# Layer 2 of a two-layer image kernel on one Trainium2 core: variances on 64 columns, and the pass towards the states reordered with its spreading step moved to GpSimd

## What is computed

```python
def _layer_norm(x, g, b):
    mu = jnp.mean(x, axis=-1, keepdims=True)
    var = jnp.mean((x - mu) ** 2, axis=-1, keepdims=True)
    return (x - mu) * jax.lax.rsqrt(var + EPS) * g + b

def _s5_block(x, i, ...):                       # x: (batch, 65536 pixels, 64 channels)
    fx = _layer_norm(x, ln1_g[i], ln1_b[i])
    h = _s5_scan(fx, ...)                       # B-matrix, a complex scan both ways, C-matrix, D * fx
    x = jax.nn.gelu(h) + fx
    fx2 = _layer_norm(x, ln2_g[i], ln2_b[i])
    return fx2 @ ff_enc[i].T @ ff_dec[i].T + fx2

x = x + _L0_conv_ref(_gn(x), ...)               # layer 1
x = x + _L1_conv_ref(_gn(x), ...)               # layer 2: _s5_block by rows and by columns, fused
```

## Time and profile before

| what | value |
|---|---|
| median of 3 runs | 9685.14 us (9671.85 to 9687.74) |
| the profiled execution | 9676.74 us, span 9674.9 us |
| TensorE busy | 8792.1 us, 91% of the span, 81958 matmul instructions |
| VectorE busy | 8178.5 us, 85% |
| ScalarE busy | 5402.5 us, 56% |
| GpSimd busy | 1604.1 us, 17% |
| mean granted TensorE clock | 0.958 of full speed |

### The profile page before, as it was taken

One profiled execution on the slowest core, in us unless ns is written; L12 is line 12 of the kernel. 1 busy time (PEld: TensorE's weight loads), 2 busy tenths in 40 slices (PEclk: granted clock), 3 DMA queues, 4 the chain that ended last, 5 costly groups with the idle time before them and its releaser, 6 DMA issues.

```text
span 9674.9 us, 203022 instructions
## 1 busy us (share of the span) xinstructions
PE 8792.1 (91%) x81958; PEld 5941.5 (61%) x81958; DVE 8178.5 (85%) x11463; ACT 5402.5 (56%) x8539; POOL 1604.1 (17%) x1824
## 2 busy tenths in 40 slices
PE   1799989999899998998989999899998999889998
PEld 1566655656566665565656666565565666656565
DVE  7799989888788988888869999887986888888786
ACT  0455546566655555556765555645675555465666
POOL 0000002333300000333320000122341000023333
PEclk6899999999999999999999999999999999999999
DMA  4777766585677777658578777756767777675755
GB/s 107 169 169 170 169 153 224 180 256 153 164 172 168 167 168 185 199 167 260 153 168 174 170 166 171 226 159 192 214 175 156 155 155 155 144 237 172 243 167 155
DMA packets 1370032, 1719.03 MB, mean 178 GB/s; under 512 B 849788, under 2 KB 1081356, under 8 KB 1283852
## 3 DMA queue, kind: packets, MB, share of 16 engines
q1 hardware_dynamic: 1369100, 1706.04, 68.9%
HBM read 852.77 MB, written 514.86 MB: 141 GB/s over the span
## 4 chain that ended last, share of the span: by engine, by line
PE 51%; SPq 19%; DMA 11%; DVE 11%; issue 4%; ACT 2%; POOL 0%; DVEq 0%; ACTq 0%; POOLq 0%
PE ps L1781 14%; SPq L788 11%; DMA H<-P 10%; PE ps L1794 7%; PE ps L1805 5%; PE ps L868 5%; PE ps L1429 3%; PE ps L882 3%; SPq L780 2%; SPq L732 2%; DVE S L1563 2%; SPq L722 2%; PE ps L1355 2%; PE ps L1388 2%; PE ps L931 2%
## 5 line engine op out<-in xcount | busy, mean ns | idle before, releaser
L1174 DVE SCALAR_TENSOR_TENSOR F<-U,LW,F 106x512 f32<-106x512 f32 x2048 | 1537.8, 751 | 63.6
L1781 PE MATMUL ps<-fp,Dwr 128*128 128x512 f32 x6144 | 1549.1, 401 | 1.9 <-DVE tt L1549 1.9
L1781 PEld LDWEIGHTS ps<-fp,Dwr 128*128 128x128 f32 x6144 | 1114.8, 188 | 618.6 <-ACT x L1870 291.3
L868 PE MATMUL ps<-P,WP 128*128 128x512 f32 x3072 | 922.4, 422 | 52.0 <-DMA H<-P 50.4
L1870 ACT ACTIVATE x<-ps,cst 128x512 f32<-128x512 f32 x512 | 352.2, 688 | 1037.2 <-PE ps L1794 1033.1
L1794 PE MATMUL ps<-XP,Cwr 128*128 128x512 f32 x3072 | 805.7, 399 | 82.4 <-DVE XP L1916 82.4
L868 PE MATMUL ps<-H,WP 128*128 128x512 f32 x3072 | 811.9, 399 | 0.0
L1042 ACT ACTIVATE xr<-P 64x1024 fp32r<-64x1024 f32 x512 | 544.0, 1063 | 475.9 <-DVE P L1143 462.1
L1927 DVE SCALAR_TENSOR_TENSOR x<-fx,g,x 128x512 f32<-128x512 f32 x512 | 382.9, 748 | 467.4 <-ACT x L1870 466.6
L1429 PE MATMUL ps<-fp,Bwr 128*128 128x512 f32 x3072 | 776.8, 403 | 0.4 <-DVE tt L1549 0.4
L1092 POOL TENSOR_SCALAR xo<-xo 64x512 f32<-64x512 f32 x4 | 6.0, 1499 | 4522.0 <-DVE xo L1208 4522.0
(11 more groups left out here) (302 smaller groups left out, 17895.0 us busy)
## 6 DMA issues: line engine op xcount, KB each, us to landing
H<-P SPq DMA_DIRECT2D x512, 585.0 KB, 7.3
raw<-x SPq DMA_DIRECT2D x240, 640.0 KB, 9.2
fx_d<-fx SPq DMA_DIRECT2D x112, 1024.0 KB, 6.6
fl_d<-fp SPq DMA_DIRECT2D x112, 1024.0 KB, 7.0
fp<-fl_d SPq DMA_DIRECT2D x112, 1024.0 KB, 6.9
fx<-fx_d SPq DMA_DIRECT2D x112, 1024.0 KB, 5.3
XT<-xT SPq DMA_DIRECT2D x256, 256.0 KB, 7.5
x1h_d<-xo SPq DMA_DIRECT2D x256, 256.0 KB, 9.2
```

What stands on the lines that cost most here:

```text
L868: e.matmul(ps[2 + i][:], w(pw_, W_CONV + 128 * j, 128), m, start=(j == 0 and pw_ == 0 and px == 0), stop=False)
L1174: ins = e.scalar_tensor_tensor(o, u, wd[0:106, i:i + 1], o, ALU.mult, ALU.add)
L1781: ins = e.matmul(bank(m)[:], Dwr[:, w, c:c + 128], fq[n % 2][x][:, s2, :], start=(s2 == 0 and w == 0 and x == 0), stop=False)
```

## The change

- `variances`: each piece's 512 columns are now cut into eight parts of 64. Two matmuls of 64 columns, with two halves of a wider `En`, fill all 32 rows of a strip where one matmul of 128 columns filled 16. The tile of a group is 128 x 64, in pass A and in pass B. The number of these matmuls doubles, their columns halve.
- the square root, `deviations` and `deviations_b` work on 64 columns in place of 128. `deviations` writes its result into a tile of its own, `rr`.
- `blocks` leaves ScalarE and becomes one `tensor_tensor` of 128 x 512 on GpSimd, ahead of the turn and the sums there.
- pass A's order on three engines: TensorE puts `bc` 0 and 1 between the first two parts of `bmm`, ahead of `center(g, 2)`, and `bc` 2 and 3 behind it; VectorE puts `norm` 0 and 1 between the two `rotate`; ScalarE does `round_` 0 and 1 behind `xcsq` 1, and `round_` 2 and 3 behind `xcsq` 3.

```diff
     def variances(e, o, i, src, pick):
-        for q in range(4):
-            ins = e.matmul(o[32 * q:32 * q + 32, 0:128], pick[:, 32 * i:32 * i + 32], src[:, 128 * q:128 * q + 128],
-                           start=(i == 0), stop=(i == 3))
+        for h in range(2):
+            for q in range(4):
+                c = 128 * q + 64 * h
+                ins = e.matmul(o[32 * q:32 * q + 32, 0:64], pick[:, 128 * h + 32 * i:128 * h + 32 * i + 32], src[:, c:c + 64],
+                               start=(i == 0 and h == 0), stop=(i == 3 and h == 1))
...
-    def deviations(e, own, done, value, out):
-        e.wait_ge(sem[done], value)
+    def deviations(e, own, f, g):
+        e.wait_ge(sem["sd"], NG * f + g + 1)
         own(e.reciprocal(rs[:], rs[:]))
         own(e.tensor_copy(rh[:], rs[:]))
-        e.scalar_tensor_tensor(rs[:], rh[:].bitcast(F32), lows, rs[:], ALU.mult, ALU.add).then_inc(sem[out], 1)
+        if g:
+            e.wait_ge(sem["rd"], NG * f + g)
+        e.scalar_tensor_tensor(rr[:], rh[:].bitcast(F32), lows, rs[:], ALU.mult, ALU.add).then_inc(sem["rs"], 1)
...
         for g in range(NG + 2):                       # TensorE
             center(g, 0)
             bmm(g - 2, 0)
+            bc(g - 1, 0)
+            bc(g - 1, 1)
             bmm(g - 2, 1)
             center(g, 2)
-            for i in range(4):
-                bc(g - 1, i)
+            bc(g - 1, 2)
+            bc(g - 1, 3)
             bmm(g - 2, 2)
             bmm(g - 2, 3)
             var(g)
...
         for g in range(NG + 1):                       # ScalarE
             xcsq(g, 0)
             xcsq(g, 1)
-            blocks(g - 1)
+            round_(g - 1, 0)
+            round_(g - 1, 1)
             xcsq(g, 2)
-            for i in range(4):
-                round_(g - 1, i)
             xcsq(g, 3)
+            round_(g - 1, 2)
+            round_(g - 1, 3)
...
-                e.activation(rs[:], ps[2][:, 0:128], ACT.Sqrt, bias=eps[:]).then_inc(sem["sd"], 1)
+                e.activation(rs[:], ps[2][:, 0:64], ACT.Sqrt, bias=eps[:]).then_inc(sem["sd"], 1)
...
             rotate(g - 3, 0)                          # VectorE
+            norm(g - 1, 0)
+            norm(g - 1, 1)
             rotate(g - 3, 1)
...
-            for i in range(4):
-                norm(g - 1, i)
+            norm(g - 1, 2)
+            norm(g - 1, 3)
             part(g - 1, 0)
             part(g - 1, 2)
             scan(g - 3)
...
     def pa_pool(e, b, d):
         f = phase(b, d)
+
+        def blocks(g):
+            e.wait_ge(sem["rs"], NG * f + g + 1)
+            if g:
+                e.wait_ge(sem["bc"], M * f + 4 * g)
+            e.tensor_tensor(RD[:].rearrange("k (q c) -> k q c", q=8), rr[:].bitcast(F32).unsqueeze(1).to_broadcast([128, 8, 64]),
+                            own_q.unsqueeze(2).to_broadcast([128, 8, 64]), ALU.mult).then_inc(sem["rd"], 1)
+
+        blocks(0)
+        blocks(1)
         for g in range(NG):
+            if g + 2 < NG:
+                blocks(g + 2)
             if g:
                 turn_pool(e, f, g - 1, slice(0, 64), 512 * g + 1, d)
```

More of the change, by code:

```diff
@@ L93, in constants @@
     k["k_ctr"] = (p[:, None] // 64 == p[None, :] // 64) * ((p[:, None] == p[None, :]) - 1.0 / 64)
-    e = np.zeros((128, 4, 32))
-    b = np.zeros((4, 32, 4, 4, 128))
-    mask = np.zeros((4, 32, 1))
+    e = np.zeros((128, 2, 4, 32))
+    b = np.zeros((8, 16, 4, 128))
+    mask = np.zeros((8, 16, 1))
     for par in range(2):
@@ L100, in constants @@
                 r = 4 * i + 2 * c + par
-                e[par * 64:par * 64 + 64, i, r] = 1.0 / 64
-                for q in range(4):
-                    b[q, r, i, q, par * 64:par * 64 + 64] = 1.0
+                for h in range(2):
+                    e[par * 64:par * 64 + 64, h, i, 16 * h + r] = 1.0 / 64
+                b[:, r, i, par * 64:par * 64 + 64] = 1.0
                 mask[:, r] = -c
-    k["k_E"] = np.concatenate([e.reshape(128, 128), mask.reshape(128, 1), np.kron(np.eye(4), np.ones((32, 1)))], 1)
-    k["k_Bc"] = np.concatenate([b.sum(3).reshape(128, 512), np.roll(b.sum(3), 64, 3).reshape(128, 512)], 1)
+    k["k_E"] = np.concatenate([e.reshape(128, 256), mask.reshape(128, 1), np.kron(np.eye(8), np.ones((16, 1)))], 1)
+    k["k_Bc"] = np.concatenate([b.reshape(128, 512), np.roll(b, 64, 3).reshape(128, 512)], 1)
     k["k_id"] = 1.0 * (p[:, None] % 64 == np.arange(64)[None, :])
@@ L135, in build @@
     ctq = at("ctq", [128, 128])
-    En, Bc = at("En", [128, 133]), at("Bc", [128, 1024], F32R)
-    lows, own_q = En[:, 128:129], En[:, 129:133]
+    En, Bc = at("En", [128, 265]), at("Bc", [128, 1024], F32R)
+    lows, own_q = En[:, 256:257], En[:, 257:265]
     RR = at("RR", [128, 2])
@@ L246, in build @@
     tiny = at("tiny", [128, 4])
-    rs = at("rs", [128, 128])
-    rh = at("rh", [128, 128], F32R)
+    rs = at("rs", [128, 64])
+    rh = at("rh", [128, 64], F32R)
+    rr = at("rr", [128, 64], F32R)
+    offset[0] += 256
     RD = at("RD", [128, 512], F32R)
@@ L1349, in deviations_b @@
         own(e.scalar_tensor_tensor(rs[:], rh[:].bitcast(F32), lows, rs[:], ALU.mult, ALU.add))
-        e.tensor_tensor(RD[:].rearrange("k (q c) -> k q c", q=4), rs[:].unsqueeze(1).to_broadcast([128, 4, 128]),
-                        own_q.unsqueeze(2).to_broadcast([128, 4, 128]), ALU.mult).then_inc(sem[out], 1)
+        e.tensor_tensor(RD[:].rearrange("k (q c) -> k q c", q=8), rs[:].unsqueeze(1).to_broadcast([128, 8, 64]),
+                        own_q.unsqueeze(2).to_broadcast([128, 8, 64]), ALU.mult).then_inc(sem[out], 1)
     def variances(e, o, i, src, pick):
-        for q in range(4):
-            ins = e.matmul(o[32 * q:32 * q + 32, 0:128], pick[:, 32 * i:32 * i + 32], src[:, 128 * q:128 * q + 128],
-                           start=(i == 0), stop=(i == 3))
+        for h in range(2):
+            for q in range(4):
+                c = 128 * q + 64 * h
+                ins = e.matmul(o[32 * q:32 * q + 32, 0:64], pick[:, 128 * h + 32 * i:128 * h + 32 * i + 32], src[:, c:c + 64],
+                               start=(i == 0 and h == 0), stop=(i == 3 and h == 1))
         return ins
@@ L1479, in round_ @@
             e.activation(piece(fp[g % 2][0], i, d), piece(fx[g % 2], i, d), ACT.Copy).then_inc(sem["f1"], 1)
[L1481 to L1489, removed]
         e.wait_ge(sem["vb"], b + 1)
@@ L1502, in pa_act @@
                 if g:
-                    e.wait_ge(sem["rd"], NG * f + g)
-                e.activation(rs[:], ps[2][:, 0:128], ACT.Sqrt, bias=eps[:]).then_inc(sem["sd"], 1)
+                    e.wait_ge(sem["rs"], NG * f + g)
+                e.activation(rs[:], ps[2][:, 0:64], ACT.Sqrt, bias=eps[:]).then_inc(sem["sd"], 1)
             if g == 1 and d and b + 1 < NB:
@@ L1571, in pa_dve @@
             if 0 <= g - 1 < NG:
-                deviations(e, own, "sd", NG * f + g, "rs")
+                deviations(e, own, f, g - 1)
             rotate(g - 3, 0)
+            norm(g - 1, 0)
+            norm(g - 1, 1)
             rotate(g - 3, 1)
@@ L1858, in pb_act @@
                     e.wait_ge(sem["rsb"], NG * f + n - 1)
-                e.activation(rs[:], ps[4][:, 0:128], ACT.Sqrt, bias=eps[:]).then_inc(sem["se"], 1)
+                e.activation(rs[:], ps[4][:, 0:64], ACT.Sqrt, bias=eps[:]).then_inc(sem["se"], 1)
                 if n < NG:
```

## The result

The changed kernel takes **9916.92 us** (median of four runs, 9911.2 to 9923.83), the kernel before beside it 9680.22: a ratio of 1.0243, with a 95% interval of 1.023 to 1.0256. It is 2.4% slower; 1.6% was forecast, and the time lies inside the range, 75 us above the forecast.

What follows compares the result with a forecast made beforehand. VectorE bounds pass A, TensorE pass B. Pass A's 150 us more, less 4 and plus 10 in pass B, make 156: 9833 against the profiled 9676.7, forecast 9842 us with the 8 us higher median, range 9735 to 9930.

Steps and rivals of the forecast that it cites:

- the ring: Pass A's middle rounds: a chain of waits through all four engines makes a round 12.84 us against 11.15.
- The wait of the second part for ScalarE: Pass A: VectorE, done by about 8.5 us, waits for ScalarE's last `round_` at 9.23; second part starts at 9.27.
- The step that failed: Pass A, TensorE: six `bmm` matmuls behind the first two `bc` take 1.45 us, so `center(g, 2)` starts at 4.55.
- The first rounds: Start of each pass A: first round -1 us, second -1.6, third +0.7.
- The ends of the passes: Pass A's last group has no `center` or squares: only the stall of 0.84 less 0.47 is left, 0.4 us.
- Pass B: Variances, TensorE's own time: 1.16 us a group for 1.08, 10 us over 128 rounds; 4 us saved at pass ends.
- The dear spread: Rival, chance 0.20: GpSimd's new operation costs 1.84 us, some 15 rounds a pass grow by 0.56, +67, 9909 us.
- The variances by instructions: Rival, chance 0.08: each variance matmul keeps 34 ns, 64 take 2.2 us, pass B's rounds grow by 1.1, 9969 us.
- the milder form: Variance matmuls start at least about 25 ns apart: 64 take 1.6 us, the sum some 65 us higher.
- Only the first stall counts: Rival, chance 0.07: the second part does not wait; pass A's middle rounds cost 0.37 us more, about 9711 us.
- VectorE's saving comes through: Rival, chance 0.04: spread, hand-overs and `bc` fit under one rotate; pass A's middle rounds take 10.68 us, about 9620 us.

Runs made afterwards that it cites:

- Experiment 2: The changed kernel with ScalarE's last two `round_` put one piece earlier, between `xcsq` 2 and 3: 9822.91 us, ratio 1.0146.
- Experiment 5: The changed kernel with VectorE's old order, `bc` 2 and 3 ahead of `center(g, 2)`, all `round_` ahead of `xcsq` 2: 9606.59 us, ratio 0.9915.
- experiment 4: The changed kernel with deviations made between the previous round's two scans, all `bc` ahead of `center(g, 2)`, all `round_` ahead of `xcsq` 2: 9782.38 us, ratio 1.0105.
- experiment 6: Experiment 5's kernel with VectorE alone in the change's order, one norm pair between the rotates: 9788.94 us, ratio 1.0104.
- experiment 7: The kernel before with only the change's order on three engines, keeping 128 columns and ScalarE's four activations into `RD`: 10083.58 us, ratio 1.0408.
- experiment 1: The changed kernel with eight matmuls, their results overwritten, put into TensorE's wait for `RD` in pass A: 9830.08 us, ratio 1.0156.
- experiment 3: The changed kernel with the old order of TensorE, ScalarE and VectorE, keeping 64 columns and GpSimd's spread: 9675.83 us, ratio 0.999.

## Why the prediction came out right, and what it lacked

- **The deviations and the ring.** Right in kind, 0.35 us long. From the reciprocal's start (2099.82) the deviations are done at 1.06 (1.10 forecast), `RD` at 2.19 (2.50), `bc` starts at 2.25 (2.60), the norm at 2.78 (3.14) with VectorE idle for 0.52 (0.84), `center(g, 2)` at 4.29 (4.55), the squares at 5.41 (5.67). The term that was most off is the spread, 1.04 us where 1.28 was taken; the hand-overs of 0.09 and 0.06 and the deviations make up the rest. A round at full clock takes 12.49 in place of 12.84.
- **The wait of the second part for ScalarE.** Its size was right where it shows, 0.72 us in the long rounds. At full clock VectorE does not wait there: ScalarE is done at 8.88 (9.23 forecast), and the first part, which the prediction has done by about 8.5, runs on to 9.03, because GpSimd's `Y` holds it up (1.97 us where 1.20 was taken). Experiment 2 showed that this part alone holds the round at 12.46. That ScalarE alone would hold it there is likely by the 8.88, but no run shows it.
- **The step that failed** is "TensorE goes on behind the first two `bc` [...] with six matmuls of `bmm`, half of 2.94 us". That duration came from a stretch with clock 1.00, in which TensorE was hardly idle. The new round makes it wait 2.3 us each time; in 74 of 96 rounds the granted clock falls at the end of that wait or soon behind it, and the six matmuls then take 1.9 to 2.8 us (2.74 in the round shown). The prediction notes a slow clock for the first round of a pass and does not ask whether the ring would make one. Measured, the middle rounds cost 96 x 1.33 = 128 us by the ring (162 forecast) and 96 x 1.18 = 113 by the clock (none forecast).
- **The first rounds.** Right in sign, gains larger: the first three fell by 1.6, by 2.45 and rose by 0.42 us, in all -29 where -15 was forecast. The ends of the passes took 11 us more where 3 was forecast.
- **Pass B.** Right. The 64 variance matmuls take 1.10 us on the timeline, 1.08 before, and the passes are 2 us longer where 10 were forecast:

```profile
1737.53 1.10 PE L1361 MATMUL ps<-sr,En 128*32 128x64 f32 x64
```

- **The rivals.** The dear spread fell: 1.04 us. The variances by instructions fell, with the milder form: 64 take 1.10 us, and their starts lie 14 ns apart on average. For that form the prediction's 65 us for 1.6 us a group hold the 10 counted already: 1.6 less 1.16 us, 128 times, is 56. "Only the first stall counts" fell by the rounds of 12.49. "VectorE's saving comes through" fell by its own condition: spread, hand-overs and `bc` were to fit under one rotate, and they are 0.09 + 1.04 + 0.06 + 0.53 = 1.72 us against 1.2. Experiment 5 gave them both rotates as cover and reached 9606.59, where the rival had 9620.

So the side was right for the reason given, and the nearness of the total owes something to two errors of opposite sign, a ring 34 us too dear and a clock of 113 us left out. That the range held the time is in part luck too: its upper end stood above 9909 for the sake of a dear spread, which did not come, and the clock filled that room.

What stays open: why the clock falls in some rounds and not in others, with the same wait of 2.3 us in both (74 of 96 here, 33 in experiment 2). With a wait of 1.83 us it fell in 34 rounds (experiment 4), with 2.09 in 38 (experiment 6), with 3.07 in 86 (experiment 7); in experiments 1, 3 and 5 and in the kernel before it fell in none.

## What to carry to other kernels

A saving on the bound engine counts only if the path that feeds it stays under its cover: draw that path through every engine it passes, and see which instructions of each list are moved in front of it. Where a new order makes TensorE wait in every round, price the matmuls behind the wait at the lower clock too. Before moving an operation to GpSimd or shifting one of its operations in time, look at what VectorE reads beside it: beside an instruction with a PSUM operand the spread took 1.04 us here, begun during one with two SBUF operands 1.95. And see which of the two begins first, for the other pays.

## What was not expected of the hardware

**The granted clock falls on short waits in a busy loop.** In a round at full clock TensorE was busy for 10.2 of 12.5 us and idle for one wait of 2.3; with the same wait, the granted clock fell to 0.50 behind it in 74 of 96 rounds. Filling the wait with work kept the clock at 1.00 (experiment 1). The Trainium skill's "TensorE: Matmul & The Clock Gate", section "What's actually happening", names two levels and ties the lower one to an idle engine; the traces agree on both levels, 0.50 and 1.00.

**GpSimd and VectorE take turns where both read two SBUF operands.** The groups by line (count, busy us, mean ns of one, idle before), of the changed kernel and then of experiment 4:

```profile
L1533 DVE TENSOR_TENSOR fp<-fx,fp 128x1024 fp32r<-128x1024 f32 x256 | 338.1, 1328 | 61.6 <-ACT fp L1487 61.6
...
L1605 POOL TENSOR_TENSOR RD<-rr,En 128x512 fp32r<-128x512 f32 x128 | 133.8, 1045 | 973.7 <-DVE rr L1345 973.7
```

```profile
L1531 DVE TENSOR_TENSOR fp<-fx,fp 128x1024 fp32r<-128x1024 f32 x256 | 422.0, 1687 | 0.0
L1603 POOL TENSOR_TENSOR RD<-rr,En 128x512 fp32r<-128x512 f32 x128 | 226.2, 1767 | 678.7 <-DVE rr L1345 678.7
```

The spread's mean goes from 1045 to 1767 ns and a part's from 1328 to 1687, with the same shapes and tiles; what differs is what runs beside them. No run put the two alone beside each other. In experiment 3, where `Y` lies mostly beside the norms, a part takes 1224 ns. The parts one by one, of the changed kernel's round at full clock and then of experiment 4, say who pays:

```profile
2106.88 1.97 DVE L1533 TENSOR_TENSOR fp<-fx,fp 128x1024 fp32r<-128x1024 f32 x1
```

```profile
2102.59 1.39 DVE L1531 TENSOR_TENSOR fp<-fx,fp 128x1024 fp32r<-128x1024 f32 x1
...
2103.91 2.31 DVE L1531 TENSOR_TENSOR fp<-fx,fp 128x1024 fp32r<-128x1024 f32 x1
```

In the changed kernel `Y` begins first (2106.47) and keeps its 1.30 us; the part ends 1.08 us behind it. In experiment 4 the `Y` of 2102.85 begins during the first part, ends 1.15 us behind that part (2105.13) and takes 2.28; the second part, begun during this `Y`, ends 1.09 us behind it. So the one that begins first keeps its time, and the other ends about its own time later, as if it had waited: in all 38 overlaps of this kind in the changed kernel the part ends 1.08 to 1.09 us after `Y`. The Trainium skill's "GPSIMD Engine Reference", section "Key points", says that GpSimd shares its SBUF interfaces with VectorE and contends with instructions that have two SBUF inputs; the trace agrees, 1.95 us beside the scan and 1.04 beside the rotate.

**GpSimd's operation on two broadcast patterns is cheaper than one on two full tiles**: 1.04 us for the spread and 1.27 to 1.30 for `Y`, both of 128 x 512 and neither held up by VectorE. The spread is a multiplication, `Y` a sum and a difference; no run parts the patterns from the operation.
